# Graph network kernel: both loads of a unit issued ahead of its column's stores, three buffers of turned counts, one unpacking moved between the last turns

## What is computed

```python
h = relu(layernorm(x))                       # no scale, no shift
for l in range(3):
    mlp  = lambda z: relu(z @ W1[l] + b1[l]) @ W2[l] + b2[l]
    msgs = mlp(h[dst])                        # one message per edge
    agg  = segment_sum(msgs, src)             # summed per source node
    h    = mlp(h + agg)
out = x + h @ Wf + bf
```

## Time and profile before

| | |
|---|---|
| runs | 2125.79, 2127.72, 2129.39 us |
| median | 2127.72 us |
| the profiled execution's own time | 2123.59 us |
| its span, first to last instruction | 2121.9 us |
| PE busy | 1957.8 us (92%) |
| DVE busy | 1403.5 us (66%) |
| ACT busy | 869.8 us (41%) |
| POOL busy | 551.1 us (26%) |
| mean granted clock of PE | 0.977 |
| bytes read from and written to DRAM | 252.58 MB, 89.89 MB |

### The profile page before, as it was taken

The page is one execution under the profiler, slowest core; times in us unless marked ns, Lnnn a source line. Parts: engine busy times, 40 slices in busy tenths (PEclk is TensorE's granted clock), DMA queues, the critical chain, the costliest instruction groups (busy, mean ns, idle before and its releaser), DMA issues.

```text
span 2121.9 us, 57789 instructions
## 1 busy us (share of the span) xinstructions
PE 1957.8 (92%) x24911; PEld 1194.8 (56%) x24911; DVE 1403.5 (66%) x1613; ACT 869.8 (41%) x2278; POOL 551.1 (26%) x270
## 2 busy tenths in 40 slices
PE   4656889999999999989999999999999999999998
PEld 3544555555555555555555555555555555555554
DVE  8999999999999999945543343343365433434333
ACT  5986999999989999922200000000010000000000
POOL 2666656666666665500000000000000000000000
PEclk9796999999999999999999999999999999999999
DMA  7356666667666666662544553543544555555452
GB/s 206 92 142 181 184 176 196 197 201 201 196 192 193 198 193 188 190 202 78 161 145 123 168 153 109 182 144 117 170 151 132 168 169 163 161 153 169 140 168 73
DMA packets 332933, 346.21 MB, mean 163 GB/s; under 512 B 21562, under 2 KB 303992, under 8 KB 332184
## 3 DMA queue, kind: packets, MB, share of 16 engines
q1 hardware_dynamic: 327516, 335.59, 54.1%
q0 software_dynamic: 2352, 6.43, 1.2%
q10 hardware_dynamic: 2816, 0.53, 0.2%
HBM read 252.58 MB, written 89.89 MB: 161 GB/s over the span
## 4 chain that ended last, share of the span: by engine, by line
PE 61%; DVE 20%; DMA 7%; issue 5%; ACT 3%; POOL 2%; SPq 2%; DVEq 0%; POOLq 0%; ACTq 0%
PE ps L1428 57%; DVE arena L766 10%; DMA arena<-counts_dram 6%; DVE arena L774 4%; POOL arena L643 2%; SPq L467 2%; DVE arena L808 2%; PE ps L1392 1%; DVE arena L813 1%; PE ps L1540 1%; PE ps L1512 1%; DMA counts_dram<-arena 1%; ACT arena L1198 1%; DVE arena L743 1%; ACT few_far L1183 1%
## 5 line engine op out<-in xcount | busy, mean ns | idle before, releaser
L1428 PE MATMUL ps<-arena,parts 128*64 128x448 fp8e4 x16464 | 1610.9, 354 | 3.8 <-DVE arena L901 1.9
L1428 PEld LDWEIGHTS ps<-arena,parts 128*64 128x64 f16 x16464 | 916.6, 110 | 655.7 <-issue 55.4
L888 DVE TENSOR_SCALAR arena<-arena 128x3136 uint16<-128x3136 uint16 x196 | 191.3, 976 | 574.7 <-PE ps L1428 574.7
L643 POOL TENSOR_TENSOR arena<-arena,weight_now 128x416 int32<-128x416 int32 x196 | 480.3, 2451 | 314.3 <-DVE arena L766 313.6
L1291 ACT ACTIVATE arena<-arena 128x448 f32<-128x448 f32 x42 | 23.9, 577 | 975.0 <-DVE arena L915 975.0
L766 DVE TENSOR_TENSOR arena<-row_iota,key_now 128x3584 f16<-128x3584 f16 (+1 forms) x196 | 403.6, 2059 | 0.0
L1198 ACT ACTIVATE arena<-ps 128x800 uint16<-128x800 f32 x392 | 342.7, 886 | 56.2 <-PE ps L1392 55.2
L1392 PE MATMUL ps<-arena 128*128 128x53 fp8e4 x6272 | 205.7, 190 | 104.9 <-POOL arena L643 88.9
L1392 PEld LDWEIGHTS ps<-arena 128*128 128x128 f16 x6272 | 187.7, 98 | 177.8 <-issue 93.2
L1183 ACT ACTIVATE few_far<-row_iota,few_now 128x128 f16<-128x128 f16 x656 | 214.1, 431 | 0.0
L774 DVE STREAM_TRANSPOSE arena<-arena 128x800 int32<-128x800 int32 x196 | 196.6, 1003 | 5.5 <-DMA counts_dram<-arena 5.5
(11 more groups left out here) (145 smaller groups left out, 841.7 us busy)
## 6 DMA issues: line engine op xcount, KB each, us to landing
arena<-counts_dram SPq DMA_DIRECT2D x294, 784.0 KB, 4.7
counts_dram<-arena SPq DMA_DIRECT2D x784, 100.0 KB, 2.3
h_dram<-parts SPq DMA_DIRECT2D x2, 1536.0 KB, 7.3
edges_dram<-arena SPq DMA_DIRECT2D x2, 1400.0 KB
arena<-in_x_dram SPq DMA_DIRECT2D x14, 192.0 KB
out_dram<-arena SPq DMA_DIRECT2D x14, 192.0 KB
arena<-in_dst_dram SPq DMA_DIRECT2D x1, 1400.0 KB
arena<-in_src_dram SPq DMA_DIRECT2D x1, 1400.0 KB
```

Of the source, the lines that this page charges most:

```text
L643: nc.gpsimd.tensor_tensor(pairs, pairs, weight_now[:, h * HW:(h + 1) * HW].unsqueeze(2).to_broadcast([P, HW, WORDS // 2]), ALU.mult).then_ ...
L888: v.tensor_scalar(spread[:, c % WIDE, 0, :].bitcast(U16), packed, 0x0F0F, None, ALU.bitwise_and)
L1428: last = t.matmul(ps[half(c), b, 0:NB], parts[:, tile, half(part)], spread[:, wide, c ^ exchange, at:at + NB].bitcast(F8), start=start and ...
```

## The change

Three edits.

1. **Loads first.** In a column whose unit opens nothing, `load_round(2u)` and `load_round(2u+1)` both stand at the head of the column's work on SP, in front of the stores of the last two groups of the column before. Columns that open a set of rows keep the old order.
2. **Three buffers.** `ctile` has three buffers (`TURNED`), so the turn of group k waits for the stores of group k-3. There are three `counts_stored` semaphores, and an opening load waits for all three. `ring0` and `spread` move up by 3200 bytes; `win` moves to the end of the arena, clear of `halves_seen`.
3. **The kept unit.** Chunk 82 is unpacked between the turns of groups 194 and 195. Its wait for the whole of unit 40 (`sums_done`) becomes one for unit 40's first chunk (`chunks_multiplied`), the last reader of that `spread` buffer.

```diff
--- before.py
+++ after.py
@@ -72,6 +72,7 @@
 CPITCH = WORDS + 2
 COLS = 2 * WORDS + 1
 PSLOTS = 2
+TURNED = 3
 LAG = 2
 WR = 6
 
@@ -229,10 +230,10 @@
         hot_r, at = view(0, [SLOTS, HW, P], F16)
         hot_c, at = view(at, [SLOTS, HW, CPITCH], F16)
         stage, at = view(at, [2, HBYTES // 2], U16)
-        ctile, build_end = view(at, [2, HBYTES], U8)
+        ctile, build_end = view(at, [TURNED, HBYTES], U8)
         ring0, at = view(build_end, [RING0, CK * SBH], U8)
         spread, at = view(at, [WIDE, 2, CK * SBH], U8)
-        win, at = view(at, [WR, 2 * WIN], I32)
+        win, at = view(ARENA - WR * 2 * WIN * 4, [WR, 2 * WIN], I32)
         assert at <= ARENA
         win_words = win.rearrange("p t c -> p (t c)")
         win_row = win_words.bitcast(F32).rearrange("p (t c f) -> p t c f", t=WR, f=2 * GRAN)[:, :, :, 0:GRAN]
@@ -293,7 +294,7 @@
             "vector_chain", "variance_made", "root_made", "h0_made", "h0_stored", "h0_turned", "h0_kept",
             "norm_made", "rows_relative", "keys_turned", "keys_kept", "cols_made", "rows_made", "few_far_found", "few_made", "hots_made",
             "batch_multiplied", "batch_kept", "counts_turned",
-                        "counts_stored_0", "counts_stored_1",
+                        "counts_stored_0", "counts_stored_1", "counts_stored_2",
             "hidden0_done", "hidden0_kept", "message0_done", "message_kept",
             "peak_found", "peak_made", "peak_shared", "peak_turned", "peak_row", "peak_spread", "scale_made", "upper_made", "parts_made",
             "counts_unpacked", "chunks_multiplied", "counts_used", "sums_kept", "sums_done", "sums_read", "u_done", "u_added", "u_kept", "own_done", "own_kept", "v_kept",
@@ -309,7 +310,7 @@
         windows_gathered = [sem(f"windows_gathered_{n}") for n in range(WR)]
         round_loaded = [sem(f"round_loaded_{r}") for r in range(RING0)]
         counts_loaded = [sem(f"counts_loaded_{r}") for r in range(RING)]
-        counts_stored = [s["counts_stored_0"], s["counts_stored_1"]]
+        counts_stored = [s["counts_stored_0"], s["counts_stored_1"], s["counts_stored_2"]]
 
         chain = [0]
 
@@ -465,14 +466,15 @@
                     for r in range(HROWS):
                         q = (d * HROWS + r) * HI
                         sp.dma_start(counts_dram[j * 2 + d, h * HW:(h + 1) * HW, r * HBYTES:(r + 1) * HBYTES],
-                                     ctile[q:q + HI, h % 2, :]).then_inc(counts_stored[h % 2], 16)
+                                     ctile[q:q + HI, k % TURNED, :]).then_inc(counts_stored[k % TURNED], 16)
 
             def load_round(n):
 
                 u, c = n // ROUND, n % ROUND
                 if c == 0 and u % SB == 0:
-                    for half in counts_stored:
-                        sp.wait_ge(half, 64 * 2 * KG * (u // SB + 1))
+                    groups = HG * KG * (u // SB + 1)
+                    for slot in range(TURNED):
+                        sp.wait_ge(counts_stored[slot], 64 * len(range(slot, groups, TURNED)))
                 if n >= RING0:
                     sp.wait_ge(s["counts_unpacked"], n - RING0 + 1)
                 sp.dma_start(ring0[:, n % RING0, :].rearrange("p (k n) -> p k n", k=CK),
@@ -483,13 +485,17 @@
                 u = unit_of(j + 1)
                 if j in (3, 6):
                     store_h0(j // 6)
+                opens = u >= 0 and u % SB == 0
+                if u >= 0 and not opens:
+                    load_round(ROUND * u)
+                    load_round(ROUND * u + 1)
                 if j:
                     store_counts(j * HG - 2)
                     store_counts(j * HG - 1)
-                if u >= 0:
+                if opens:
                     load_round(ROUND * u)
                 store_counts(j * HG)
-                if u >= 0:
+                if opens:
                     load_round(ROUND * u + 1)
                 store_counts(j * HG + 1)
             store_counts(BUILD * HG - 2)
@@ -769,9 +775,9 @@
             def turn_counts(k):
 
                 dve.wait_ge(s["batch_kept"], 2 * k + 2)
-                if k >= 2:
-                    dve.wait_ge(counts_stored[k % 2], 64 * (k // 2))
-                v.transpose(ctile[:, k % 2, :].bitcast(I32), stage[:, k % 2, :].bitcast(I32)).then_inc(s["counts_turned"], 1)
+                if k >= TURNED:
+                    dve.wait_ge(counts_stored[k % TURNED], 64 * (k // TURNED))
+                v.transpose(ctile[:, k % TURNED, :].bitcast(I32), stage[:, k % 2, :].bitcast(I32)).then_inc(s["counts_turned"], 1)
 
             def make_hots(k):
                 j, h, slot = k // HG, k % HG, k % SLOTS
@@ -866,6 +872,8 @@
                 dve.wait_ge(round_loaded[n % RING0], 16 * (n // RING0 + 1))
                 if c == 0 and u > FUSED:
                     dve.wait_ge(s["counts_used"], u - FUSED)
+                elif c == 0:
+                    dve.wait_ge(s["chunks_multiplied"], u)
                 else:
                     dve.wait_ge(s["sums_done"], SBB * u)
                 packed = ring0[:, n % RING0, :].bitcast(U16)
@@ -1007,11 +1015,10 @@
                     dve.wait_ge(s["weights_fused"], 1)
                     v.tensor_tensor(bf_last[:], bfrow[:], ps[:, 2, 3 * P + L:3 * P + L + D], ALU.add).then_inc(
                         s["weights_fused"], 1)
-            for k in range(BUILD * HG - LAG, BUILD * HG):
-                turn_counts(k)
-
-
+
+            turn_counts(BUILD * HG - 2)
             unpack_tail(ROUND * FUSED)
+            turn_counts(BUILD * HG - 1)
             unpack_tail(ROUND * FUSED + 1)
             unpack_tail(ROUND * FUSED + 2)
             for i in range(SB):
```

## The result

| | before | changed |
|---|---|---|
| median of 4 runs | 2128.19 us | 2105.59 us |
| runs | 2125.79 to 2129.39 | 2104.39 to 2106.24 |
| the profiled execution's own time | 2123.59 us | 2106.24 us |
| its span | 2121.9 us | 2104.5 us |
| DVE busy | 1403.5 us | 1402.2 us |

The ratio is 0.9895, 95% interval [0.9877, 0.9912]: faster by 1.05%. 2110.1 us was forecast, with a range of 2103.5 to 2118.0. The profiled pair differs by 17.35 us, where the sum made against it had 17.6. The medians differ by 22.6 us; against 2127.72 us, the median of three runs on which the forecast stood, it is 22.1.

The account below looks back on a forecast made before the run. The build was taken as set by DVE and its waits; 10.8 + 0.6 + 4.4 + 1.8 = 17.6 us off 2123.59 us gave 2106.0, and a median of 2110.1 us, range 2103.5 to 2118.0.

Parts of the forecast that it names:

- Loads first: In the build's ordinary columns, 16 waits for odd loads go, 10.8 us, plus a 0.55 us wait for PE: 11.4 us.
- Three buffers: In the build's columns, turns wait for no stores, with 11.6 us of cover; 0 us saved there.
- the sum made against it: Whole kernel: 10.8 + 0.6 + 4.4 + 1.8 = 17.6 us off the profiled execution's 2123.59 us, giving 2106.0.
- The 7.4 us for two buffers: In the build's columns, time from one turn's end to the turn that waits for its stores, with two buffers.
- The end: At the end of the build, `add_kept` starts at about 912.5 instead of 916.94: 4.4 us earlier.
- The clock: At and behind `add_kept`, PE no longer runs at half clock after its idle 5.15 us: 1.8 us.
- I take it that the clock stays: At the end of the build, PE idles about 0.7 us and keeps full clock: 1.8 us.
- the median should go from 2127.7 to 2110.1: Whole kernel: the profiled execution lay 4.1 us under the median of the runs, so 2106.0 became 2110.1 us.
- Stores too late: Rival, ordinary columns: stores landing over 11.6 us behind their turn make DVE wait, 36 us per microsecond over; chance 0.03.
- The pace: Rival, build columns: pace passes to PE, `unpack_low` waits for it, only the end's 6.2 us left: 2121.5; chance 0.06.
- The end gave all it had: Rival, build's end: late next load or falling clock leaves 0 to 4.4 us there: 2111.9 to 2116.3; chance 0.10.

Follow-up runs that it names:

- the second set: Changed kernel run again, unchanged, beside kernels with two of the three edits, on another chip: median 2107.09 us, ratio 0.9905 to the kernel before.

## Why the prediction was right, and where a size was off

- **Loads first: right.** I took 10.8 us from 16 waits, plus 0.55 us for PE. The 16 waits are gone, and the opening columns kept theirs. My reason for them was too mild, though: the median landing of 5.4 us mixes even and odd loads. Odd ones alone took 6.7 us in the median, wanted after 6.6, so being late was common, 16 times in 36. The 11.3 us at most was a load behind the build; in the columns none took over 8.7. The columns gave 709.0 - 694.9 = 14.2 us between the first and the last `unpack_low`, 2.8 us more than my 11.4. 0.3 us of it are smaller waits in opening columns, 0.55 us are waits for PE (they fell from 1.95 to 0.85 us, and I had taken 0.55). Nearly 2 us are left. 1.4 of them come from a term I did not have, in the last section; the rest is open.
- **The profiled pair: near, and partly by luck.** The first `unpack_low` came 1.1 us later than before, in a stretch that the change does not touch; so 14.2 + 4.35 - 1.1 make up the 17.4 us between the profiled pair, and the clock's 1.8 us of my sum are not in it. That 17.35 is so near 17.6 is luck: 2.8 us taken too little in the columns stand against 1.8 for the clock and 1.1 ahead of the first unpacking.
- **Three buffers: right.** No turn waits for stores in the columns. I had the stores behind two loads at 2.3 to 11.3 us; they landed 7.1 us behind their turn in the median. The 7.4 us for two buffers were wrong, the cover there is 8.3. The runs add what the trace of before could not show: with loads first two buffers do nearly the same, so the third one is a reserve and hardly a gain.
- **The end: right.** 4.4 us were forecast and 4.35 came. Chunk 84 was in time.
- **The clock: mis-sized.** I took 1.8 us for PE's half clock behind its idle 5.15 us, and that execution did pay 1.7. The gap at the same place cost 2.6 and 2.8 us in two further executions of before, so the term was read from one execution at its low end. "I take it that the clock stays" is the step that failed in the profiled pair. At `add_kept` it stayed in both traces of the changed kernel, but the gap of 1.95 us at 1008 us cost 1.7 us in one of them, so the term came to nothing there.
- **The median: 4.5 us too high.** The step that failed is "the median should go from 2127.7 to 2110.1", which carried the profiled execution's distance to the median, 4.1 us, over to the changed kernel. I had priced it at up to 4 us for the range and left it out of the point. The changed kernel's profiled execution lies at its own runs (2106.24 among 2104.39 to 2106.24), and so did the two further ones of before (2126.21 and 2126.12 us, with medians of 2125.8 and 2126.54). A part is the few runs: over 61 runs before had medians of 2125.7 to 2127.05 and not 2127.7, and in the second set the change was worth 18.6 us. That the rest of the distance was part of what the change removes is likely and not shown. What is shown is that the kernel before varies: in the kernels that keep the loads' places, the waits in ordinary columns went from 7.3 to 18.0 us and the clock's price from 1.7 to 2.8 us; 10 runs of the changed kernel lie within 4.2 us, where sets of 10 to 12 runs of before span 8.5, 8.5 and 18.9. That the late loads made the single runs near 2137 us was not seen, since no such run was profiled.
- **The rivals.** Stores too late: shown to exist, at 2 us or more beyond the slowest stores of the changed kernel. The pace did not pass to PE: DVE's waits for it in the columns fell. The end gave all it had in the build, and the clock's part was lost again at 1008 us.

## What to carry to other kernels

A prefetch that is issued 6.6 us before it is wanted and lands in 5.1 to 8.7 us, as the odd loads did, is a gamble in each iteration, and the cost of such gambles varies between executions: compare the profiled time with the spread of the runs before taking its waits as the size of the gain. Read such a landing time by kind of load, since a median over all of them can hide the late ones. Putting a load in front of stores on one queue is cheap as long as the stores' buffers have time; read that time at the group that stands behind the loads (here 8.3 us with two, 11.6 with three) and hold it against how long after their turn its stores land (here 7.1 us in the median, 9.6 at most) before adding a buffer. A wait for "all stores so far" is worth reading again: here the even chunk needed four columns of seven, and that was 5.8 us.

## What the runs showed of the hardware that I had not expected

- A wait costs more than its idle row says. In the kernel before a column with a wait of 0.28 us took 17.22 us, one with 1.60 us took 18.55 us and one with 2.06 us took 19.00 us, where a column without one takes 16.86: 0.08 or 0.09 us more than the idle time each. Instructions of DVE that don't wait overlap the one before by about that much (878.79 + 0.97 reaches past the next one's start at 879.67), and one that waited doesn't. Over 16 waits this is 1.4 us of the 2 that my sum lacked.
- Behind an idle gap PE ran at full clock first and at half clock after, or at half clock at once, or not at half clock at all, with gaps of nearly the same length: 5.15 and 5.57 us cost 1.7 and 2.6 us, one of 4.08 us cost 2.8 us, one of 2.08 us 1.8 us and another of 2.08 us nothing, 2.26 us nothing. A gap of 1.93 to 1.95 us, some 110 us behind `add_kept`, stands in all 14 profiled executions; the clock fell behind it in three (1.7 us each) and stayed in eleven.
- The DMA engines took 72 more loads of 784 KB in the build (226 to 303 GB/s in the slices there instead of 164 to 224) at little cost with three buffers. The columns took 705.1 us from the first to the last `unpack_low` instead of 694.9. Of these 10 us 4.5 are turns that waited for stores, and 1.3 are longer waits for the opening loads; the rest is open. With two buffers the same traffic cost 107.6 us of waits for stores.
